# Indirect loads released step by step by TensorE's progress in a DLRM tower with a CIN layer

## The reference

```python
e = jnp.stack([tbl_0[ids[:, 0]], ..., tbl_31[ids[:, 31]]], axis=1)     # (1024, 32, 32)
x = e
for W in (W0, W1):                                                     # (1024, 128), (4096, 128)
    z = jnp.einsum('bhd,bmd->bhmd', e, x).reshape(b, -1, 32)
    x = jnp.einsum('bpd,pj->bjd', z, W)
    res.append(x)
z = jnp.sum(jnp.concatenate(res, axis=1), axis=-1)                     # (1024, 256)
h = jnp.concatenate([z, dense_ctx], axis=1)
h = jnp.maximum(h @ W_top1 + b_top1, 0.0)
h = jnp.maximum(h @ W_top2 + b_top2, 0.0)
y = h @ W_top3                                                         # (1024, 1)
```

## Time and profile before

| | us |
|---|---|
| median of 3 runs | 378.07 |
| lowest, highest | 377.61, 382.9 |
| span of the profiled execution | 597.7 |
| PE busy (matmuls) in that execution | 412.6 |
| ACT busy | 235.5 |
| DVE busy | 203.4 |
| POOL busy | 246.5 |

### The profile page before, as it was taken

One profiled execution on the slowest core, in us unless ns is written; L12 is line 12 of the kernel. 1 busy time (PEld: TensorE's weight loads), 2 busy tenths in 40 slices (PEclk: granted clock), 3 DMA queues, 4 the chain that ended last, 5 costly groups with the idle time before them and its releaser, 6 DMA issues.

```text
span 597.7 us, 9512 instructions
## 1 busy us (share of the span) xinstructions
PE 412.6 (69%) x3656; PEld 360.8 (60%) x3656; DVE 203.4 (34%) x834; ACT 235.5 (39%) x774; POOL 246.5 (41%) x262
## 2 busy tenths in 40 slices
PE   5512112874257887877788778687787679999988
PEld 4301001653256776766666667577676668989988
DVE  4200000694723333322333233333332235556510
ACT  3300000662175334522343334433452237676641
POOL 6777772547055444544445554544444440000000
PEclk9755555795589877877787888977787779999999
DMA  8100000000000000000000000000000000000000
GB/s 299 45 14 13 13 13 6 11 3 14 2 10 10 8 10 7 10 8 9 9 9 10 10 10 9 11 8 9 8 10 8 8 10 2 2 2 2 2 2 1
DMA packets 10765, 9.66 MB, mean 16 GB/s; under 512 B 4664, under 2 KB 8896, under 8 KB 10720
## 3 DMA queue, kind: packets, MB, share of 16 engines
q0 software_dynamic: 8192, 4.21, 4.8%
q1 hardware_dynamic: 2528, 4.84, 2.3%
HBM read 9.03 MB, written 0.00 MB: 15 GB/s over the span
## 4 chain that ended last, share of the span: by engine, by line
PE 57%; issue 18%; another core or an unknown queue 11%; DVE 7%; ACT 6%; DMA 1%; SPq 0%; ACTq 0%
PE WA L725 20%; PE QB L697 10%; PE PA L687 8%; PE T L710 4%; DVE RT L421 4%; PE M L738 4%; PE M L757 2%; PE ET L674 2%; ACT eblk L285 2%; ACT TS L285 1%; PE PA L639 1%; PE M L764 1%; PE M L748 1%; ACT RT L285 1%
## 5 line engine op out<-in xcount | busy, mean ns | idle before, releaser
L278 POOL DMA_INDIRECT emb<-in_table,rows x256 | 245.8, 960 | 239.0 <-PE ET L674 165.3
L725 PE MATMUL WA<-TS,RX 128*128 128x128 f32 x896 | 127.0, 301 | 1.0 <-ACT TS L285 1.0
L584 DVE COPY TS<-T 32x64 f32<-32x64 f32 x256 | 55.5, 217 | 200.6 <-PE T L710 184.6
L725 PEld LDWEIGHTS WA<-TS,RX 128*128 128x128 f32 x896 | 119.7, 215 | 6.0 <-issue 6.0
L697 PE MATMUL QB<-eblk,zQ 128*64 128x68 f32 x1024 | 69.1, 243 | 74.3 <-issue 74.0
L697 PEld LDWEIGHTS QB<-eblk,zQ 128*64 128x64 f32 x1024 | 49.9, 146 | 89.8 <-issue 85.8
L552 DVE TENSOR_TENSOR zQ<-ET,eT 128x1024 f32<-128x1024 f32 x32 | 39.2, 1225 | 159.0 <-ACT eT L285 158.9
L687 PE MATMUL PA<-eblk,zP 128*128 128x132 f32 x512 | 80.6, 296 | 5.3 <-issue 3.4
L639 PE MATMUL PA<-sym,TS 128*128 128x272 f32 x64 | 29.4, 552 | 74.5 <-issue 47.3
L687 PEld LDWEIGHTS PA<-eblk,zP 128*128 128x128 f32 x512 | 73.4, 212 | 6.3 <-issue 4.9
L285 ACT ACTIVATE eblk<-ET 32x256 f32<-32x256 f32 x128 | 48.6, 380 | 71.0 <-PE ET L674 66.0
(11 more groups left out here) (87 smaller groups left out, 294.1 us busy)
## 6 DMA issues: line engine op xcount, KB each, us to landing
emb<-in_table,rows POOLq DMA_INDIRECT x256
TS<-in_W SPq DMA_DIRECT2D x8, 256.0 KB, 4.3
wt<-in_W_top SPq DMA_DIRECT2D x2, 512.0 KB
y1w<-in_W_rows SPq DMA_DIRECT2D x1, 448.0 KB
TS<-in_W_rows SPq DMA_DIRECT2D x1, 448.0 KB
sym<-in_W_cols SPq DMA_DIRECT2D x1, 264.0 KB, 2.8
TS<-in_W_cols SPq DMA_DIRECT2D x1, 264.0 KB, 3.1
idc<-in_ids SPq DMA_DIRECT2D x1, 128.0 KB, 2.0
```

Of the source, the lines that this page charges most:

```text
L278: eng.indirect_dma_start(emb[par][:, g, :], None, table, bass.IndirectOffsetOnAxis(rows[:, k, g:g + 1], 0))\
L584: eng.tensor_copy(view(ts[32 * q:32 * q + 32, :, :], P * REST + b0, [[4 * P, 2], [P, 4], [1, 8]]), view(src, q, [[C17, 2], [4, 4], [C33, 8 ...
L725: m = eng.matmul(WA[:, 0:P], C[:, kt, :], TS[k % 2][:, slot_of(kt), :], start=(kt == 0), stop=(kt == KT - 1))
```

## The change

POOL's loop over the loads gets a wait ahead of a load, which depends on its number n alone. Loads 0 to 15 have none. Each of loads 16 to 27 waits for two more weight products of PE (load 16 for 2, load 27 for 24). From load 28 on the loads are counted in eights: the first six of eight go in pairs, each pair behind one trio of unit u = (n - 28) // 8, and the last pair goes behind `other_triples` of that unit. All loads, their order, their destinations and their existing waits stay; no other engine's queue is changed.

```diff
+        FREE = 16
...
+            def gate(n):
+
+                if FREE <= n < FREE + F // 2 - 4:
+                    eng.wait_ge(rt_made, 2 * (n - FREE) + 2)
+                if n >= FREE + F // 2 - 4:
+                    u, j = divmod(n - FREE - F // 2 + 4, UG)
+                    if j < 2 * TRIOS:
+                        if j % 2 == 0:
+                            eng.wait_ge(p_made, TRIOS * u + j // 2 + 1)
+                    elif j == 2 * TRIOS:
+                        eng.wait_ge(t3_made, u + 1)
+
...
                     for g in range(UG * unit, UG * unit + UG):
+                        gate(P // NQ * k + g)
                         eng.indirect_dma_start(emb[par][:, g, :], None, table,
```

## The result

The changed kernel takes 381.22 us (median of 20 runs), the kernel before 377.54 us in the same comparison: ratio 1.0097, 95% interval 1.0077 to 1.0117. It is 3.7 us slower, and that is within 2%. Ratios and their intervals leave out the few runs that lie over 1.5% above the fastest of their kernel.

The account below looks back on a forecast made before the run. It took nearly all the starvation to be the profile's alone, with POOL and PE tied at 325 us. 90 + 254 + 22 = 366 us, 12 around it, and 5 for lost lead gave 383 us, range 373 to 391.

Parts of the forecast that it names:

- The 5 us of the forecast: Time the waits on POOL's loads add to the run, taken between ends of 0 and 13.5 us.
- The clean sum of 366 us: Kernel before without starvation: second tile starts at 90 us, seven tiles take 254, the end 22; sum 366 us.
- 12 us for what lies around the span and for anything left out: Whole kernel before: what the median run leaves beyond the summed 366 us, so nearly all starvation belongs to the profiled execution.
- The tie at 325 us: End of POOL's loads before the change: POOL ends at 324 us, PE needs the last unit's loads at 325.
- The mixed case of the prediction: Whole run at 1.25 us a load and 5 us of DVE hold-up: span 372 before, 379.5 after, 7.5 more.
- The price of a load: POOL's loads: 0.94 us busy plus 0.30 between loads, 1.25 us each.
- the rule that POOL never gets its lead back: Loads 60 to 255: a unit's eight loads take POOL 10.0 us, PE needs 9.08, so POOL's own pace counts.
- the two ways out that the prediction left: Kernel before, 385 us with full hold-up: either a load costs 1.21 us or less, or DVE's hold-up is partial.
- The gates' loss: Loads 28 to 60: load 60 waits until 91.5 us instead of going at 79, taking 12 us of POOL's lead.
- The rival of POOL as the bound: Loads to the end: 1.25 us each holds in timed runs, DVE's hold-up is small; 386 to 391.5 us, chance 0.32.
- The rival of starvation: PE beside runs of loads: part of the starvation is in timed runs, spreading gives 9 to 14 us; chance 0.14.
- The forecast of the profile after: Changed kernel's profile: span 420 to 470 us, units of 11 to 12 us, no 8 us waits at L639.

Follow-up runs that it names:

- g_late: The kernel before with only the change's waits from load 60 on, none on earlier loads; ratio 1.0093 against the kernel before, profiled span 381.3 us.

## Why the prediction was right, and where it was not

- **The forecast.** Within 2%, 383 us, range 373 to 391; measured 381.22. The direction of the small move was right as well. The 5 us of the forecast were chosen between 0 and 13.5, not added up. With the 9 to 11 us of hold-up that the profiles show, the prediction's own terms give 1.5 to 3.5 us (a gate at 91.5 us, load 60 at 88 to 90 without it), so the closeness of 383 is partly luck.
- **The clean sum of 366 us** was right: 366.6 with the loads' bound taken away. That it came from a profile disturbed by 220 us, from stretches without hold-up, shows that such a profile can still be read. Two of its terms cancelled, though: in that kernel the last sum ends at 71.6 us, not 75, and PE takes 18.6 us from there to the second tile, not 15.
- **"12 us for what lies around the span and for anything left out"** was the mis-sized step. Around the span lie 1.8 us. The other nine to ten (366.6 us against a median span of 375.4, or 10.3 by the prediction's 378.07) were PE waiting for rows behind POOL: the kernel before was bound by POOL already.
- **The tie at 325 us** failed for that reason. It left DVE's hold-up out of POOL's sum before the change and then put 0 to 18 us in as a bound. The first profile couldn't show it, as its sums came after load 60. The later profiles have 9 to 11 us of it: without a gate load 60 goes at 88 to 90 us, not at 79, and POOL ends at 335 instead of 324. The mixed case of the prediction, 1.25 us a load and 5 us of hold-up, had the right form and half the hold-up.
- **The price of a load**, 1.25 us, holds: 195 loads in 243.4 us are 1.248 each, and so does the rule that POOL never gets its lead back. Of the two ways out that the prediction left, a cheaper load or a partial hold-up by DVE, it was the second.
- **The gates' loss** of 12 us of lead, cut to a total of 5, was measured as 3.7. The gate on load 60 was put at 91.5 us; load 60 goes at 90.1 to 94.3 us in the five profiles with these gates. Part of that is the clock of PE in the weight transposes. Load 28 waits 0.5 to 4.2 us beyond the usual gap, where 4 was said. The prediction looked at load 60 alone; the profiles lose the lead at loads 28, 54 to 56 and 60, in changing parts.
- **The rival of POOL as the bound** named the mechanism that the runs show, at a price that they don't: it asked for a small hold-up by DVE, and 8 us or more. Its condition was false and its mechanism true, before the change as well as after. The forecast counted it as a separate case when it was the frame of all cases.
- **The rival of starvation** fell. No profile but the first shows it.
- **The forecast of the profile after** was wrong where it spoke of the hold-up: a span of 420 to 470 us, units of 11 to 12 us and a service time of up to 1.5 us a load were read from a disturbance as if it followed the loads. The span is 377.0 with loads at 1.25 us throughout. The signs for POOL as the bound came true: gaps of 0.3 us, and PE waiting for "DMA emb".
- **The Trainium skill.** That a DVE instruction with two SBUF inputs contends with a GpSimd instruction that reads SBUF (SBUF — State Buffer, Who interferes with whom) agrees with the profiles, where a load beside such sums took up to 11.94 us instead of 0.94. The sentence on records of instructions (NOTIFIC — the notification-queue block) was no help: the twelve profiled executions after the first have spans of 366.6 to 390.3 us and none is held up, so records alone don't explain the first.

**Open.** What stretched the first profile. What brings the low clock from 82 to 90 us in some executions, and whether it is the cause of the longer ones; the attempt to fill the idle time ahead of it didn't decide it. Why a load beside the same sums takes 0.94 us in one place and 11.94 in another. Whether a gate makes the long hold-ups by DVE more frequent; they come with gates and without.

## What to carry to other kernels

Before gating a queue, ask whether its engine has time to spare over the whole run: if it issues without a pause to the end and the others wait for it, its first idle microsecond is in the total, and the gate is harmless only if it is met (here, with eight loads more of lead). A sum made from stretches that a disturbance left alone is worth more than the disturbed profile, but what the disturbance moved apart (here DVE's sums and the loads) is missing from it; and when it comes out 10 us short of the timed run, look for a second bound before calling the difference overhead. Have a suspicious profile taken again before explaining it.

## What the runs showed of the hardware

- An indirect load of 128 rows of 128 bytes costs POOL 1.248 us, 0.94 busy and 0.30 between two; a met wait ahead of it adds nothing that the rows show.
- Beside DVE's instructions with two SBUF operands most loads take 1.0 to 2.6 us, single ones 3.5 and 4.6, two to five a profile their usual 0.94, and at times a load doesn't end before the row of sums does: 4.13, 7.18 and 11.94 us. Beside products with one operand in PSUM it takes 0.94 to 0.96.
- The rows land 2.4 us after the issue (median of the changed kernel), 3.7 at most there.
- With the same work in PE's queue, the granted clock from 82 to 90 us is 1.00 (2.4 GHz) in the profile of the changed kernel and 0.51 (1.2 GHz) in that of g_late, and the first tile takes 3.1 us longer in the second.
- One profiled execution was 220 us longer than the median of those timed, with POOL at its usual pace and PE and ACT starved beside it.
